# A vision-transformer tower on one core: eighteen stages moved by one or two slots in a hand-written order

## What is computed

```python
h = concat(cls_tok, resize8x8(haar_maps(x)) @ W + b)       # 64 images x 65 tokens x 64 channels
h = h + attention(layernorm(h))                            # 8 heads, cosine scores, position bias, softmax
q = layernorm(h) @ Wq                                      # 8 heads x 64
s0, s1 = (layernorm(h) @ Wq_pk) . pk_keys                  # per head 64 + 64 product-key scores
top = top16 of s0[i] + s1[j] over the best 16 of each      # 16 of 4096 rows of a table, per token and head
w = softmax(top); k = sum w * keys_table[rows]; v = sum w * values_table[rows]
h = h + (softmax(q k^T + causal) v) @ Wo                   # causal attention over the 65 tokens
```

## Time and profile before

| | |
|---|---|
| median of 3 runs | 2952.06 us (2951.39 to 2952.8) |
| profiled execution | 2948.71 us |
| its span (first to last instruction) | 2946.9 us |
| first unit's spread starts at | 138.2 us |
| busy: PE, PEld, DVE, ACT, POOL | 2853.7, 1976.2, 2512.6, 1769.7, 1586.5 us |
| masks (L1250) | 2560, mean 530 ns, 1346.3 us |
| unit exponentials (L1028) | 2560, mean 475 ns, 1179.3 us |

### The profile page before, as it was taken

The page is one execution under the profiler, slowest core; times in us unless marked ns, Lnnn a source line. Parts: engine busy times, 40 slices in busy tenths (PEclk is TensorE's granted clock), DMA queues, the critical chain, the costliest instruction groups (busy, mean ns, idle before and its releaser), DMA issues.

```text
span 2946.9 us, 60045 instructions
## 1 busy us (share of the span) xinstructions
PE 2853.7 (97%) x16560; PEld 1976.2 (67%) x16560; DVE 2512.6 (85%) x10266; ACT 1769.7 (60%) x4888; POOL 1586.5 (54%) x3427
## 2 busy tenths in 40 slices
PE   8899999999999999999999999999999999999998
PEld 7867766666666666666666666666666666777776
DVE  4678889998899889988998899989998998788876
ACT  4466666565656656665566565655566666666665
POOL 2234456665666556655666566656665665343331
PEclk9999999999999999999999999999999999999999
DMA  9213211112111211121212111211121111101100
GB/s 219 55 47 82 54 30 32 33 34 43 29 33 34 41 26 33 34 42 30 34 34 41 32 33 34 40 33 33 34 39 33 34 35 35 26 21 27 26 21 19
DMA packets 121290, 117.48 MB, mean 40 GB/s; under 512 B 61491, under 2 KB 109310, under 8 KB 120958
## 3 DMA queue, kind: packets, MB, share of 16 engines
q1 hardware_dynamic: 105525, 83.84, 13.5%
q0 software_dynamic: 14336, 29.39, 5.9%
q10 hardware_dynamic: 1096, 0.41, 0.1%
HBM read 66.36 MB, written 9.84 MB: 26 GB/s over the span
## 4 chain that ended last, share of the span: by engine, by line
PE 72%; DVE 18%; issue 5%; POOL 3%; ACT 2%; ACTq 0%; DMA 0%; DVEq 0%; POOLq 0%
PE ps L854 40%; PE ps L840 14%; DVE wts L1250 7%; DVE x_sum L1325 3%; PE ps L776 2%; PE ps L804 2%; PE ps L885 2%; PE ps L745 2%; PE ps L727 1%; PE ps L793 1%; PE ps L869 1%; ACT wts L1028 1%; PE ps L767 1%; DVE top L1234 1%; DVE cand_rest L1236 1%
## 5 line engine op out<-in xcount | busy, mean ns | idle before, releaser
L854 PE MATMUL ps<-wts,table 128*128 128x455 f32 (+2 forms) x5120 | 2004.9, 475 | 0.0
L1250 DVE SCALAR_TENSOR_TENSOR wts<-ps,wts 128x455 f32<-128x455 f32 (+2 forms) x2560 | 1346.3, 530 | 280.3 <-ACT wts L1028 266.6
L1028 ACT ACTIVATE wts<-ps 128x455 f32<-128x455 f32 (+2 forms) x2560 | 1179.3, 475 | 368.2 <-PE ps L840 346.0
L840 PE MATMUL ps<-st,spread 128*128 128x456 f32 (+2 forms) x2560 | 1288.6, 503 | 36.2 <-DVE wts L1250 28.5
L854 PEld LDWEIGHTS ps<-wts,table 128*128 128x128 f32 x5120 | 906.6, 190 | 141.4 <-issue 62.9
L840 PEld LDWEIGHTS ps<-st,spread 128*128 128x128 f32 x2560 | 483.9, 189 | 400.1 <-DVE wts L1250 268.5
L612 POOL DMA_INDIRECT x_rows<-folded,x_r x448 | 452.8, 1011 | 87.1 <-issue 78.7
L545 POOL TENSOR_SCALAR stat<-top 110x1 f32<-110x1 f32 (+1 forms) x268 | 70.0, 261 | 717.7 <-DVE top L1234 715.0
L532 POOL TENSOR_TENSOR cand<-best 110x15 f32<-110x15 f32 (+5 forms) x804 | 159.9, 226 | 178.1 <-DVE best L1218 176.6
L1325 DVE SCALAR_TENSOR_TENSOR x_sum<-iota,x_pf,x_at 128x69 f32<-128x69 f32 x448 | 179.3, 400 | 0.0
L804 PEld LDWEIGHTS ps<-ident,parts 110*128 110x128 f32 (+1 forms) x536 | 63.3, 141 | 139.4 <-issue 121.0
(11 more groups left out here) (188 smaller groups left out, 3839.2 us busy)
## 6 DMA issues: line engine op xcount, KB each, us to landing
st<-st SPq DMA_DIRECT2D x320, 114.0 KB
table<-in_table SPq DMA_DIRECT2D x128, 128.0 KB, 4.4
rz_row<-rz_dram SPq DMA_DIRECT2D x52, 165.0 KB
folded<-table SPq DMA_DIRECT2D x64, 128.0 KB, 2.6
x_rows<-folded,x_r POOLq DMA_INDIRECT x448
rz_row<-rz_dram SPq DMA_DIRECT2D x28, 228.0 KB
scratch<-in_x SPq DMA_DIRECT2D x7, 343.0 KB
rz_dram<-rz SPq DMA_DIRECT2D x52, 1.3 KB
```

Of the source, the lines that this page charges most:

```text
L840: mm(ps[0:128, g % NA, 0:t], spread[:, q * 128:(q + 1) * 128], st[:, k % 2, ORDER[c // QUADS], 0:t], start=True, stop=True).then_inc(a_rea ...
L854: mm(ps[0:128, ACC + k % 2, 0:t], table[:, k % H, i, :], wts[:, g % RING, 0:t], start=(c == 0), stop=(c == CH - 1)).then_inc(out_done, 1)
L1028: A(wts[:, g % RING, 0:t], ps[0:128, g % NA, 0:t], ACT.Exp).then_inc(e_ready, 1)
L1250: V.scalar_tensor_tensor(out=wts[:, g % RING, 0:t], in0=ps[0:128, g % NA, 0:t], scalar=0.0, in1=wts[:, g % RING, 0:t], op0=ALU.is_ge, op1= ...
```

## The change

It moves instructions to other slots, and adds or removes none. Sizes, buffers and operands are untouched; so is every semaphore wait.

- Tile search: best-of-16 steps to 3, 4, 5 (from 2, 3, 5); the five steps of top24 to 7 to 11 (from 8 to 12); upper parts 16 (15); lower parts 17 (16); transposes 18 (17); `st` copy 20 (19); reciprocal 15 (16).
- Picks: first search 3 to 7 (from 2 to 6); gathers from 23 on (from 22).
- First attention: PE scores at -1 (from 0), exponential at 6 (5), PE output at 9 (11); projection one slot earlier.
- Second attention: value transposes 5 (6), exponential 9 (8), transposes 12 (13), add to h 18 (17); `take_sum` at u = 2 (1).

```diff
--- before.py
+++ after.py
@@ -95,16 +95,16 @@
 
 TILE_START = {CH * (k - 1) - 16 + 8 * (t + sparse(k)): (k, t) for k in range(HEADS) for t in range(tiles(k))}
 PICK_START = {CH * (k - 1) - 16: j for j, k in enumerate(PICKS)}
-OUT, BEST, CAND, TOP, SHIFT, ZSUM, HIGH, ZINV, LOW, TURN, TURNED = 2, (2, 3, 5), 6, 8, 13, 15, 15, 16, 16, 17, 19
+OUT, BEST, CAND, TOP, SHIFT, ZSUM, HIGH, ZINV, LOW, TURN, TURNED = 2, (3, 4, 5), 6, 7, 13, 15, 16, 15, 17, 18, 20
 
 ROWS = 22
 MAPS, TOK, LN1 = ROWS + 3, ROWS + 6, ROWS + 10
 QK, VAL, NRM, ATT = LN1 + 11, LN1 + 14, LN1 + 17, LN1 + 28
 PERIOD = 16
 
-X_OUT, X_BEST, X_CAND, X_INDEX, X_WHERE, X_TOP = 1, 2, 7, 8, 9, 9
+X_OUT, X_BEST, X_CAND, X_INDEX, X_WHERE, X_TOP = 1, 3, 7, 8, 9, 9
 X_NEG, X_WEIGHT, X_POS, X_ZINV, X_NORM, X_ROW, X_FOUND = 13, 14, 15, 16, 17, 17, 21
-X_GATHER, X_ADD, X_TURN, X_MOVE = 22, 30, 77, 78
+X_GATHER, X_ADD, X_TURN, X_MOVE = 23, 30, 77, 78
 
 GROUPS = CH * H // 4
 FOLD, FOLD_EARLY, FOLD_LATE = ROWS, 45, 211
@@ -718,7 +718,7 @@
                     for b in range(n):
                         last = tr(of_image(ps[0:128, FR, :], b), inv[:, b, :], ident[0:L, 0:L])
                     last.then_inc(nrm_turned, 1)
-                j = task_at(p, q, 0)
+                j = task_at(p, q, -1)
                 if j is not None:
                     pe.wait_ge(kx_ready, base + j + 1)
                     if j >= 1:
@@ -736,7 +736,7 @@
                         last = tr(of_image(ps[0:L, bank("weights", p), :], b), of_image(expo[:, j % 2, :], b),
                                   ident[0:L, 0:L])
                     last.then_inc(pt_mm, 1)
-                j = task_at(p, q, 11)
+                j = task_at(p, q, 9)
                 if j is not None:
                     pe.wait_ge(pt_out, base + j + 1)
                     if j >= 1:
@@ -750,7 +750,7 @@
                     for b in range(n):
                         last = tr(of_image(ps[0:C, FR, :], b), o_tok[:, b, :], ident[0:L, 0:L])
                     last.then_inc(ot_mm, 1)
-                if q == after_tasks(p) + 3:
+                if q == after_tasks(p) + 2:
                     pe.wait_ge(ot_out, p + 1)
                     mm(ps[0:128, FR, 0:t], w_proj[:, :], hx[:, 0:t], start=True, stop=True).then_inc(proj_mm, 1)
                 layernorm(p, q, 1, after_tasks(p) + 8)
@@ -868,12 +868,12 @@
                     for b in range(n):
                         last = mm(of_image(ps[0:L, AT, :], b), of_image(xh, b), of_image(kv, b), start=True, stop=True)
                     last.then_inc(s2_mm, 1)
-                if u == 6:
+                if u == 5:
                     pe.wait_ge(s2_add, a + 1)
                     for b in range(n):
                         last = tr(ps[0:L, AT, b * C:(b + 1) * C], of_image(kv[C:128, :], b), ident[C:128, C:128])
                     last.then_inc(v2_mm, 1)
-                if u == 13:
+                if u == 12:
                     pe.wait_ge(p2_ready, a + 1)
                     pe.wait_ge(v2_out, a + 1)
                     for b in range(n):
@@ -968,7 +968,7 @@
                 if q == NRM + 1:
                     act.wait_ge(nrm_mm, p + 1)
                     A(nrm[:, 0:n * 2 * H], ps[0:L, FR, 0:n * 2 * H], ACT.Sqrt).then_inc(nrm_ready, 1)
-                j = task_at(p, q, 5)
+                j = task_at(p, q, 6)
                 if j is not None:
                     act.wait_ge(s_sub, base + j + 1)
                     A(expo[:, j % 2, 0:t], expo[:, j % 2, 0:t], ACT.Exp).then_inc(s_exp, 1)
@@ -1032,7 +1032,7 @@
                 if u == 7:
                     act.wait_ge(v2_mm, a + 1)
                     A(v2[:, 0:n * C], ps[0:L, AT, 0:n * C], ACT.Copy).then_inc(v2_out, 1)
-                if u == 8:
+                if u == 9:
                     act.wait_ge(s2_sub, a + 1)
                     A(s2[:, 0:n * L], s2[:, 0:n * L], ACT.Exp).then_inc(s2_exp, 1)
                 if u == 15:
@@ -1278,7 +1278,7 @@
                 if u == 10:
                     dve.wait_ge(s2_sum, a + 1)
                     V.reciprocal(red2[:, 1, 0:n], red2[:, 1, 0:n]).then_inc(s2_inv, 1)
-                if u == 17:
+                if u == 18:
                     dve.wait_ge(o2_mm, a + 1)
                     if a % H == 0:
                         dve.wait_ge(h_moved, a // H + 1)
@@ -1380,7 +1380,7 @@
             for g, k, u, p, q in slots():
                 if 0 <= g < UNITS:
                     mask_unit(g)
-                if k >= 1 and u == 1:
+                if k >= 1 and u == 2:
                     take_sum(k - 1)
                 if tile_at(g, ZINV):
                     invert_sum(*tile_at(g, ZINV))
```

## The result

The kernel after takes 2839.65 us (median of 4 runs, 2838.72 to 2840.09) against 2952.15 before: a ratio of 0.9619 (95% interval 0.9602 to 0.9635), 112.5 us faster. The forecast was 2925 with a range of 2896 to 2960: right in sign, four times too small in size (27 us), and the measured time lies outside the range. The profiled execution has a span of 2838.1 us.

The account below looks back on a forecast made before the run. PE was taken as first bound, but not alone, with DVE near. Terms of -30 + 2 + 1 = -27 us against the profiled 2948.71 gave 2921.7; the median, 3.35 above that execution, was forecast at 2925, range 2896 to 2960.

Parts of the forecast that it names:

- DVE's waits for PE: DVE's waits at the bias add, add to h and normalization: all taken to go, 57.6 us of DVE idle.
- kx for the scores at -1: New wait in POOL's queue, 14 tasks 0.6 us late: taken as 0, ends 0 and 8 us.
- POOL's product: New wait of the second attention's transposes at 12 in heads 3 and 5: 2 us, ends 0 and 13.
- The wait of top24 for the candidates: New wait of top24 at 7 for candidates at 6: old and new waits cancel, 1 us taken.
- the bound: Rival: POOL bounds the dependent steps, candidates late for top24 at 7; 2986 us, or 2963 with a third; chance 0.13.
- The reciprocal at 15: Tile search's reciprocal in the softmax sum's slot: costs 0 with an earlier threshold.
- DVE's waits for exponentials: Mask waits for ACT's exponential after the tile search: 59 us of DVE idle removed, ends nothing and 118 us.
- I cost all of these at nothing: Other edits: take_sum, value transposes, st copy, gathers, projection; margins suffice, 0 us.
- a rival on the other side: Collisions of DVE and POOL: x_sum lengthened beside kx, 36 us of DVE, 9 of the end; 2934 us; chance 0.04.
- this exponential: ACT's exponential at u = 0, 8, 16, 24, standing behind softmax sum and upper parts, which wait for POOL's threshold.
- 0.26: Price of a microsecond of DVE idle in us of the end: 117 us give 30; ends 0 and 1.
- the no-change rival: PE is full at 97%, masks' waits only its slack: 2952 us, 2955 at most; chance 0.14.

Follow-up runs that it names:

- e10: The kernel after with the picks' gathers back at slot 22: ratio 0.9761 to the kernel before, 42 us slower than the kernel after.
- e12: The kernel before with the tile-search slots moved and the gathers at 23, attentions unchanged: ratio 0.9755, 31 us faster than e1.
- e16: e1 with POOL's second-attention instructions put ahead of the picks' in the same slot, no slot changed: ratio 0.9747, 34 us faster than e1.
- e1: The kernel before with only the tile-search slots moved: ratio 0.9861 to the kernel before, -41 us.
- e5: The kernel before with only the tile search's transposes at 18 instead of 17 and the st copy at 20 instead of 19: ratio 0.9950, -15 us.
- e6: The kernel after with upper parts back at 15 and lower parts back at 16: ratio 0.9625 to the kernel before.
- e13: The kernel before with 320 spare DVE instructions (70.0 us busy) behind the masks at u = 3, 11, 19, 27: ratio 1.0064, 19 us slower.
- e7: e1 plus the first attention's four edits, second attention, take_sum and picks as before: ratio 0.9882 to the kernel before.
- e9: The kernel after with the first attention back in its old slots: ratio 0.9720 to the kernel before.

## Why the prediction was wrong

*Right.* No work was added; the granted clock stayed. DVE's waits for PE went nearly as forecast: 57.6 to 13 us. kx for the scores at -1 costs nothing (PE shows no wait for it); that POOL's earlier start is the reason was not tried. PE's weight loads wait for POOL's product 8.4 us (L880; 3.0 before), where I took 2. The wait of top24 for the candidates went from 12.9 to 18.0 us, not to 60, so POOL did not become the bound. The reciprocal at 15 costs 4.5 us of waiting. DVE's waits for exponentials fell by 75 us; I had said 59, but for a reason that holds only in part (see the third step).

*A wrong label.* The stretches of the earlier trace rows are not heads 28 and 29. In those heads DVE is idle for 2.1 and 3.2 us, not 3.1 and 2.4. Their lengths, and so the 1.27 and 1.07 us for a slot, are right, and the sum uses none of the busy times.

*The step that failed.* "I cost all of these at nothing", said of the gathers: "gathers have 7 slots instead of 8 for a transfer". I looked at when a gather must have landed, and not at which of POOL's instructions it stands next to. This edit is worth 42 us in the kernel after (e10) and 31 on the tile search (e12), and it works by the mechanism that I had as a rival on the other side. "One more for each of 28 picks is 28 x 1.3 = 36 us of DVE" had the right amount with the wrong sign: the long ones were taken away, 37 us of x_sum's busy time. Its price, 9 us of the end, was about four times too low. I also named the wrong neighbour. I had kx beside the long x_sum; kx accounts for 1.4 of the 56 us in excess and the subtraction L571 for 33. The Trainium skill (SBUF — State Buffer, Who interferes with whom) says that a DVE instruction with two SBUF inputs and a GpSimd instruction that reads SBUF exclude each other; the ends of x_sum with L571 in e10 and in e16 agree. It says that the order of issue decides who blocks; in e10 x_sum started 0.77 us ahead of L571 and yet ended behind it. An issue alone did not hold it (0.28 us, e1), but why it loses its turn to a subtraction right behind one stays open.

*The second.* PE's own wait at the transposes was in none of my terms. It was in the view of waits, as 121.0 us by "issue" on PE's weight loads, and I read the name as "nothing". It was worth 15 us (e5).

*The third.* "The change takes upper parts from in front of this exponential", 59 us of idle time at 0.26, 15 us of the end: this edit moves 20 us of that waiting and is worth nothing measurable in the kernel after (e6). The rest of the 75 us came by other edits, mostly of the tile search (95 us in e1); which ones was not tried.

*The price.* The 0.26 was right in one slot (0.27 in e13). Used as one price for all it was wrong: 0.05 in another slot, about 1 for the blocked x_sum. And it let me add the parts up, as though they were independent. They are not: the first attention is worth nothing (e7) or 30 us (e9) by what else has been done.

*What stays open.* The gathers' 42 us and the transposes' 15 are 57 of the 85 us that the forecast lacked, if they add up. The other 26 us of the tile search were not taken apart.

*The ceiling.* A PE that is "full at 97%" was the ground of the no-change rival. The busy figure did not move much, 2853.7 of 2946.9 to 2778.5 of 2838.1, but 75 us of "busy" went with no matmul fewer and rows no shorter in sum: the durations of all matmul rows add up to 5803 us before and 5853 after. Busy counts a time covered by several rows once, and the rows, whose ends are modelled, overlap more in the kernel after. The Trainium skill calls that figure a bad metric (Trainium Kernel Development and Optimization, Performance Expectations), and the trace agrees. Its own measure, the weight loads' share, says 71% now, and 26.02 of 38.99 us in a dense head in which PE's rows show no idle time; what told the two kernels apart was the chain, 72% and 93% over PE.

## What to carry to other kernels

In a schedule written by slots, what an edit does to an engine's *neighbours in order* counts as much as what it does to due times: list for every moved instruction which instructions of the other engines it now runs beside. An instruction whose longest time is six times its median has a story; match its ends with the other engines' ends before pricing it. And do not price all stalls alike: here a microsecond in pieces of 0.2 us cost 0.05 to 0.27 us, and one in blocks for which a second engine waits too cost about 1.

## What the hardware showed

A DVE instruction of 0.28 us took 1.85 us while POOL issued an indirect DMA (1.10 us) and then read SBUF (0.96 us); with the two in the other order it took 0.64 us. 61 of the same instructions that began during such an issue with nothing right behind it took 0.28 us on average (e1). "issue" as the releaser of PE's weight loads can hide a wait for a semaphore: at 157 of 268 tiles it was ACT's copy, ended 0.22 us earlier. The same 16560 matmul instructions showed 75 us less busy time though their rows were no shorter in sum (5803 and 5853 us), since they overlap more.
